# Recurrent layers of a graph network: which of a step's sixteen one-hot tiles the scalar engine makes, two (8th, 16th) or three (5th, 10th, 16th)

## The reference, cut to what matters

```
def gcn(x, W, b):
    xw = x @ W
    agg = jax.ops.segment_sum(nw[:, None] * xw[src], dst, num_segments=n)
    return agg + b
...
for l in range(conv_w.shape[0]):            # 3 layers
    x = out
    I = sigmoid(gcn(x, Wl[0], bl[0]) + gcn(H, Wl[1], bl[1]) + wc[l, 0] * C + bg[l, 0])
    F = sigmoid(...); T = tanh(...); C = F * C + I * T
    O = sigmoid(gcn(x, Wl[6], bl[6]) + gcn(H, Wl[7], bl[7]) + wc[l, 2] * C + bg[l, 3])
    out = O * tanh(C)
```

## Time and profile before

| | before |
|---|---|
| time, median of 3 runs | 9894.26 us (9861.93 to 9896.99) |
| the profiled execution, time / span | 9950.19 us / 9948.5 us |
| granted PE clock, mean over the span | 0.879 |
| busy: PE, DVE, ACT, POOL (share of span) | 63%, 68%, 39%, 31% |
| DVE one-hots, line 1778: count, busy, mean | 2436, 794.7 us, 380 ns |
| ACT copies of found rows, line 1746: count, busy, mean | 696, 337.7 us, 485 ns |
| PE adds, line 1689 with DVE's one-hots: count, mean | 2436, 398 ns |

### The profile page before, as it was taken

How to read it: one execution, slowest core, us unless ns; L and a number is a source line. 1 busy time by engine, 2 the same in 40 slices (tenths; PEclk the granted TensorE clock), 3 DMA queues, 4 the chain that set the end, 5 groups by cost and what they waited for, 6 DMA issues and landing times. The chain is left out here.

```text
span 9948.5 us, 140910 instructions
## 1 busy us (share of the span) xinstructions
PE 6270.1 (63%) x41452; PEld 3103.4 (31%) x41922; DVE 6734.8 (68%) x11389; ACT 3919.7 (39%) x5017; POOL 3064.5 (31%) x2943
## 2 busy tenths in 40 slices
PE   3100120059878787978879787977777777455555
PEld 2100110025334333433334343433343434222222
DVE  8864650048778777877778787878897979533333
ACT  0000000012455554545545554544676757223223
POOL 0047437730233232323223232333000000455553
PEclk9999975579899898989989898988999999677777
DMA  2000000034667665766667676766211212101110
GB/s 80 3 13 1 4 22 9 5 91 140 211 202 227 203 218 196 229 204 209 217 198 233 201 225 198 228 199 194 67 58 61 64 52 64 20 18 25 22 21 24
DMA packets 493714, 1158.29 MB, mean 116 GB/s; under 512 B 115153, under 2 KB 150649, under 8 KB 492678
## 3 DMA queue, kind: packets, MB, share of 16 engines
q1 hardware_dynamic: 241952, 815.85, 25.7%
q10 hardware_dynamic: 157440, 298.89, 8.5%
q0 software_dynamic: 93568, 33.84, 2.7%
HBM read 932.28 MB, written 216.20 MB: 115 GB/s over the span
## 5 line engine op out<-in xcount | busy, mean ns | idle before, releaser
L1404 PE MATMUL acc<-dst_hot,parts 128*128 128x512 bf16 x11130 | 2918.2, 388 | 666.5 <-issue 430.2
L1463 ACT ACTIVATE parts_out<-acc 96x1024 bf16<-96x1024 f32 x2320 | 2339.9, 1020 | 2080.6 <-PE acc L1415 1773.9
L1367 POOL DMA_INDIRECT group_best<-best_dram,best_row x1250 | 1352.2, 1082 | 3079.7 <-SPq L1331 2775.3
L1279 DVE TENSOR_SCALAR dst_hot<-dst_rows,node_f 128x2048 bf16<-128x2048 int16 x2910 | 2052.1, 740 | 235.3 <-PE acc L1415 180.1
L1404 PEld LDWEIGHTS acc<-dst_hot,parts 128*128 x11600 | 1057.8, 99 | 1904.7 <-issue 804.7
L909 POOL DMA_INDIRECT gathered<-table_dram,source_index x719 | 729.4, 1014 | 2143.5 <-POOLq L153 1629.4
L304 POOL DMA_INDIRECT got<-edges_dram,record_index x928 | 952.7, 1027 | 850.1 <-DVEq L772 548.5
L1689 PE MATMUL sums_by_dst<-dst_hots,edge_message 128*96 128x512 bf16 x2436 | 879.6, 398 | 283.5 <-DVE dst_hots L1778 280.5
L1415 PE MATMUL acc<-source,parts 128*128 128x128 bf16 x9280 | 924.6, 223 | 8.8 <-issue 5.2
L1415 PEld LDWEIGHTS acc<-source,parts 128*128 x9280 | 642.0, 99 | 645.5 <-issue 380.9
L1778 DVE TENSOR_SCALAR dst_hots<-node_row,dst_col 128x640 bf16<-128x640 int16 x2436 | 794.7, 380 | 30.4
(11 more groups left out here) (373 smaller groups left out, 8030.9 us busy)
## 6 DMA issues: line engine op xcount, KB each, us to landing
dst_rows<-step_dst_dram SPq DMA_DIRECT2D x582, 512.0 KB, 5.2
source<-source_dram SPq DMA_DIRECT2D x582, 512.0 KB, 8.5
best_dram<-best_out ACTq DMA_DIRECT2D x580, 256.0 KB
factor<-step_weight_dram ACTq DMA_DIRECT2D x560, 256.0 KB
sources<-source_dram SPq DMA_DIRECT2D x174, 512.0 KB, 3.6
src_rows<-step_src_dram SPq DMA_DIRECT2D x58, 512.0 KB
source_dram<-source_made SPq DMA_DIRECT2D x58, 512.0 KB
group_best<-best_dram,best_row POOLq DMA_INDIRECT x1250
```

Of the source, the lines that this page charges most:

```text
L1279: nc.vector.tensor_scalar(hot[k % 2][b][:, :], index_rows[k % 3][:, :], node_f[:, b:b + 1], None, ALU.is_equal).then_inc(hot_ready, 1)
L1367: pool.indirect_dma_start(group_best[:, g, h, :], None, best_dram, bass.IndirectOffsetOnAxis(ap=best_row[:, i:i + 1], axis=0)).then_inc(en ...
L1404: nc.tensor.matmul(acc[n % 3][:, 0:TILE], blocks[b], hot[k % 2][b][:, q * TILE:(q + 1) * TILE], start=(b == 0), stop=(b == DST_BLOCKS - 1))
L1463: act.activation(moved[n % (2 * QUADS)][:, :], acc[n % 3][0:SPLIT, :], ACT.Copy).then_inc(tile_moved, 1)
```

## The change

One tuple. ACT makes the one-hots of i = 4, 9 and 15 in place of 7 and 15; DVE makes the other thirteen in place of fourteen: it takes on i = 7 and gives up i = 4 and 9. ACT's list gets a third pair per step, behind the copy of q = 2, between the first and the second cast. act_dst_hot grows from four buffers to six, of 640 bf16 values per partition each. PE's waits for i = 4, 7 and 9 change their semaphore accordingly. The ring of eight stays.

```
-            ACT_SUBS = (7, 15)
+            ACT_SUBS = (4, 9, 15)
             DVE_SUBS = tuple(i for i in range(STEP_SUBS) if i not in ACT_SUBS)
             HOTS2 = 8
```

## The result

The changed kernel takes 9923.26 us (median of 8 runs, 9911.86 to 9931.21); the kernel before 9887.04 us (8 runs, 9861.63 to 9896.99). The ratio is 1.0041, 95% interval 1.0028 to 1.0054: slower by 36 to 41 us. Forecast was +37 us.

A forecast was written before the change was run, and what follows sets the result against it. A loop through DVE, PE and ACT was taken as the bound, 8.21 us a step; a longer one of 8.41 gave 168 x 0.20 = 34 us, plus 3: +37 us, 9894 to 9931 us. Range for 8 in 10: 9888 to 9966.

The forecast's parts named there:

- The bound is a loop, not DVE: A ring through ACT's copies and first cast, DVE's line 1795 and PE's findings sets the step, 8.21 us.
- Rival 1: DVE is the bound: the step gets 0.30 us shorter, 51 us faster over 174 steps, 9843 us; chance 0.10.
- DVE's saving is worth 0: One one-hot less ahead of line 1795 only lengthens DVE's 0.66 us stall there by 0.30; gain 0.
- rival 3: Slower still: quarter 2's 0.13 us slack or others fail, step 0.33 to 0.40 longer, about 9958 us; chance 0.22.
- loop B: Ring from copy 1 through ACT's third pair, second cast, line 1798 and quarter 1's finding: 8.41 us, +0.20 a step.
- The second cast comes late, line 1798 waits: ACT's third pair delays the second cast; line 1798 on DVE waits 0.3 to 0.4 us a step, some 60 us.
- Start and end of the layers: Each layer's second iteration costs at most 1.2 us, three times; trailing steps about -0.3 each; together +3 us.
- Rival 2: No change: the old loop stays longer if 0.35 us cast lateness shrinks to 0.19 slack; 9894 us; chance 0.16.
- The stall ahead of line 1795 grows to 0.8 to 0.9: DVE's wait at line 1795 for ACT's first cast: 0.8 to 0.9 us a step instead of 0.66.
- Copy 1 waits for quarter 1 by a little; copy 3 doesn't wait: On ACT, the wait for quarter 3 is gone and the wait for quarter 1 is new and small.
- Rule 1 of the Trainium skill: Giving work to ACT may pay where DVE is saturated; by it the change would be worth rival 1's 51 us.
- no change: Outcome class for the whole kernel: measurement tells about 0.5% (49 us) from no change; chance of same 0.58.

The follow-up runs named there:

- one_less: The kernel before, with nobody making the one-hot of i = 4 (DVE thirteen, ACT still two pairs); ratio to before 1.0001.
- two_0_3: The kernel before, with ACT's second pair moved from behind copy 1 to behind copy 3, same work; ratio to before 0.9882.
- three_0_c0_3: The changed kernel, with ACT's three pairs behind copy 0, the first cast and copy 3; ratio to the kernel before 0.9869.
- t9_copy3: The changed kernel, with ACT's third pair moved from behind copy 2 to behind copy 3; ratio to the kernel before 1.0070.

## Why the prediction was right, by its steps

- *The bound is a loop, not DVE.* Right: 8.21 us before; one_less takes away a one-hot without moving the layers by 0.1 us; two_0_3 moves one pair, the stall goes, and the layers gain 124 us. Rival 1's price had a slip: 0.30 x 174 is 52 us, not 51 (51 is right for the unrounded 0.293).
- *DVE's saving is worth 0.* Right where I put it (DVE's stall ahead of line 1795), but incomplete. The saved one-hot is worth nothing by itself and 0.19 us a step next to the third pair, because it keeps copy 2 off its wait. I had the slack (0.13) as rival 3 and the 0.30 that makes it, but counted the edit "worth 0". The net of +0.22 is +0.41 for the pair and -0.19 for i = 4. The forecast holds all the same, since the sum of loop B already has quarter 2 found 0.30 earlier.
- *The second cast comes late, line 1798 waits.* Right, with a size a little too large: it was expected to wait 0.3 to 0.4 us a step, some 60 us in all; it waits 0.27 to 0.32 in the steps shown, 50.6 us in all. The second cast no longer waits, as expected.
- *Loop B 8.41.* 8.43 in the step shown, 8.44 in the median. 0.22 a step instead of 0.20. None of its ten distances is off by more than 0.02, so the sum isn't right by errors that cancel. Start and end of the layers: +3 forecast; line 1798's first wait in a layer grows to 1.69 us in the trace, from 0.69 before, and so does the first step of each layer, by about 1.0. Three of these and 168 x 0.22 make 40 us; measured in the layers, 39.5. Rival 2 asked for too little: for no change loop B would have to be 0.20 shorter, the difference of the two sums, and not 0.16.
- *The stall ahead of line 1795 grows to 0.8 to 0.9.* It is 0.77 in most steps, 141.9 us in 171 waits (0.83) over all; before it was 0.68 over all.
- *Copy 1 waits for quarter 1 by a little; copy 3 doesn't wait.* Right: copy 1 (7154.30) starts 0.37 behind the finding, the shortest distance in these rows, and 0.85 behind its forerunner on ACT (7153.45), where the cast at 7156.24 follows the same kind of instruction by 0.64. The profile gives copy 1 no bracket in that step, so its wait is read from these distances. Copy 3 follows the second cast by 0.52, as an instruction without a wait does.
- *Rule 1 of the Trainium skill* (Perfetto Trace Analysis, Optimizing Scalar/DVE Operations: offload when DVE is saturated): in the kernel before, 90% busy was not saturated; one_less shows it. In two_0_3 DVE is at 98%, and three_0_c0_3, which gives it one one-hot less and ACT one pair more, gains 4.7 us in the layers and nothing that the times tell: there the ring through ACT's casts closes next.
- *The whole.* +37 us forecast; measured +36 by medians, 0.41% by the ratio, +39.5 in the layers. It lies inside the 0.5% that I had put as the bound of "no change" (0.58). That bound was too wide: with eight runs of each kernel the interval is 0.28% to 0.54%, clear of zero.

What stays open: what makes the granted clock fall in sixteen steps of t9_copy3. And three_0_c0_3 against two_0_3 isn't settled in whole time.

## What to carry to other kernels

Where engines wait for each other in a ring, the highest busy share need not name the bound: here 90% didn't, and 98% did. Write down the start-to-start distances around the ring, and ask of each edit which segment it stands in. An instruction in an in-order list costs what is queued behind it: here the same 1.55 us pair costs 0.71 us a step more behind copy 1 than behind copy 3. Before work is given to an engine that "has time", look at where in its list the idle time is. Here reordering that list was worth three times what the change cost.

## What was not expected of the hardware

In these traces an instruction that finds its inputs ready starts before its forerunner on the engine ends: DVE's line 1797 in two_0_3 starts 0.89 us into a run of three one-hots of 0.97 us. Where it has to wait, that overlap is lost as well: in the earlier trace rows line 1795 starts 1.62 us behind the start of three such one-hots, which is their 0.97 and the stall of 0.66 with nothing taken off. So the stall costs some 0.08 us more than its bracket says: the step fell by 0.71 us when a stall of 0.58 to 0.66 in most steps went.

PE's granted clock can fall in the middle of steady work: in the four of t9_copy3's sixteen long steps whose course was read (from 7060.14, 7069.63, 7206.96 and 7783.91) it stands at 0.50, the lower of its two levels, for some 3 us, and a 512-column add takes 0.63 us in place of 0.38.
